# Attention and routing stage of a two-layer kernel: hand-written instruction orders with an earlier routing, one activation table, pads split over two queues, first expert weights scaled by ScalarE

## The reference, cut to what matters

```python
q, k = softplus(q), softplus(k)                          # 16 heads of 8
kv  = cumsum(k[:, :, :, None] * v[:, :, None, :], axis=1)
num = einsum('zsD,zsDe->zse', q, kv)
den = sum(q * cumsum(k, axis=1), axis=-1, keepdims=True)
x   = x + gate * ((num / den) @ Wo.T + bo)               # residual sum
t   = h * rsqrt(mean(h*h) + eps) * norm_scale            # h: layer norm of x, modulated
top_v, top_i = top_k(t @ gate_w + gate_b, 2)             # routing
probs = softmax(top_v)
y   = sum over the two experts of probs * (swiglu(t @ w1 + b1) @ w2 + b2)
out = x + gate * (h + y)
```

## Time and profile before

| | |
|---|---|
| device time, median of 3 runs | 1131.31 us (1131.22 to 1132.76) |
| the profiled execution, first to last instruction | 1130.5 us |
| PE, DVE, ACT, POOL busy | 904.8, 863.6, 682.1, 563.3 us |

### The profile page before, as it was taken

The page is one execution under the profiler, slowest core; times in us unless marked ns, Lnnn a source line. Parts: engine busy times, 40 slices in busy tenths (PEclk is TensorE's granted clock), DMA queues, the critical chain, the costliest instruction groups (busy, mean ns, idle before and its releaser), DMA issues.

```text
span 1130.5 us, 21078 instructions
## 1 busy us (share of the span) xinstructions
PE 904.8 (80%) x6543; PEld 700.5 (62%) x6543; DVE 863.6 (76%) x2224; ACT 682.1 (60%) x1756; POOL 563.3 (50%) x567
## 2 busy tenths in 40 slices
PE   4997799279999949999999999942088888888820
PEld 4994377134445438888888888831077777777710
DVE  2776788789998866788999999955467777676748
ACT  1357510689996376688988987755055555555510
POOL 1121000656885224433888888856635655555530
PEclk9999899579999969999999999975589999999975
DMA  7000233123333132000101111111242222222148
GB/s 191 14 1 5 75 112 112 52 85 132 123 118 113 75 102 51 2 8 9 42 32 39 38 37 40 35 37 45 82 131 72 82 71 77 79 68 77 45 165 307
DMA packets 72002, 84.37 MB, mean 75 GB/s; under 512 B 18182, under 2 KB 59841, under 8 KB 69716
## 3 DMA queue, kind: packets, MB, share of 16 engines
q1 hardware_dynamic: 52564, 60.60, 17.1%
q0 software_dynamic: 8704, 18.11, 4.8%
q10 hardware_dynamic: 10624, 4.33, 1.4%
HBM read 59.33 MB, written 23.67 MB: 73 GB/s over the span
## 4 chain that ended last, share of the span: by engine, by line
PE 39%; DVE 9%; issue 5%; ACT 4%; another core or an unknown queue 3%; DMA 1%; SPq 1%; POOL 0%; DVEq 0%; ACTq 0%; POOLq 0%
PE ps L2086 9%; PE ps L2304 9%; PE ps L2102 3%; PE ps L2323 3%; DVE qk L2003 2%; PE ps L2077 1%; PE ps L2064 1%; PE ps L2051 1%; PE ps L2097 1%; PE ps L2191 1%; PE ps L2156 1%; PE ps L2145 1%; PE ps L2209 1%; DVE qk L2008 1%
## 5 line engine op out<-in xcount | busy, mean ns | idle before, releaser
L1399 POOL DMA_INDIRECT rows_of<-payb,posu x128 | 143.2, 1119 | 53.3 <-issue 28.7
L1390 POOL TENSOR_TENSOR kvb<-qk,v 128x1024 f32<-128x1024 f32 x64 | 126.4, 1980 | 86.4 <-DVE qk L1756 53.0
L1032 PE MATMUL ps<-masked,ew 128*128 128x512 f32 x256 | 129.6, 621 | 4.2 <-DVE masked L960 3.5
L2086 PE MATMUL ps<-con,kvb 128*128 128x128 f32 x1024 | 126.9, 278 | 0.0
L2086 PEld LDWEIGHTS ps<-con,kvb 128*128 128x128 f32 x1024 | 120.4, 193 | 0.7 <-issue 0.7
L1424 POOL DMA_INDIRECT parts<-h,dest x72 | 74.0, 1028 | 72.3 <-ACT h L1658 47.2
L1649 ACT ACTIVATE nrm<-qk 128x512 f32<-128x512 f32 x72 | 45.4, 630 | 101.3 <-DVE qk L2003 87.8
L1424 POOL DMA_INDIRECT parts<-gx,dest x72 | 73.6, 1022 | 55.0 <-ACT gx L1658 33.9
L960 DVE TENSOR_TENSOR masked<-f_t,wide 128x512 f32<-128x512 f32 x128 | 88.9, 712 | 9.2 <-PE ps L1032 8.9
L1732 DVE TENSOR_TENSOR qc<-ps,qk 128x1024 f32<-128x1024 f32 x64 | 77.9, 1217 | 18.1 <-PE ps L2086 17.7
L2304 PE MATMUL ps<-qd,ex 128*128 128x256 f32 x288 | 74.4, 405 | 18.0 <-ACT ex L1634 15.8
(11 more groups left out here) (355 smaller groups left out, 2444.1 us busy)
## 6 DMA issues: line engine op xcount, KB each, us to landing
wide<-hot_dram SPq DMA_DIRECT2D x16, 1024.0 KB, 4.6
kvb<-rows_of SPq DMA_DIRECT2D x72, 132.0 KB
toep<-taps_dram SPq DMA_DIRECT2D x16, 512.0 KB, 3.8
out_dram<-x_tok ACTq DMA_DIRECT2D x16, 256.0 KB, 5.6
rows<-rows_dram SPq DMA_DIRECT2D x16, 192.0 KB, 3.1
kvb<-parts SPq DMA_DIRECT2D x6, 512.0 KB, 7.2
rows<-rows_dram SPq DMA_DIRECT2D x16, 128.0 KB, 4.4
xg<-in_w_dram SPq DMA_DIRECT2D x1, 2048.0 KB, 9.7
```

Source lines behind the costliest of these rows:

```text
L1032: nc.tensor.matmul(ps[:, w % 2, :], ew0[:, e, :], masked[e % 4][:, :], start=False, stop=(e == E - 1)).then_inc(s["product"], 1)
L1390: nc.gpsimd.tensor_tensor(kv[g % KB][:, :, :].rearrange("p e (h d) -> p e h d", h=H), k_in, v_in, ALU.mult).then_inc(s["kv"], 1)
L1399: nc.gpsimd.indirect_dma_start(rows_of, bass.IndirectOffsetOnAxis(ap=posu[w % 2][:, slot, t:t + 1], axis=0), pay[w % PB][:, t, :], None).t ...
L2086: last = nc.tensor.matmul(cum(g)[:, e, :], kv[g % KB][:, e, :], k("upto"), start=True, stop=True)
```

## The change

1. The round loops of POOL, ACT, DVE and PE are replaced by orders that are written out call by call. Routing runs closer behind the residual sum: in a steady round DVE calls `residual`, `moments`, `shifted`, `modulated` and `gated` of the same window, and `logits` to `placed` of the window two before. POOL makes the four products of window w in a row and then the eight sends of window w - 4 in a row; sends begin behind window 4 (before: behind window 6).
2. PE's waits for the shared banks are counted from what has been issued (`issued[...]`); waits for `abs_q` and `abs_k` are added. ACT's `relu_queries` waits for `den` too, its `relu_keys` for `kv`, `st_ps` and `k1` in place of `red`.
3. ACT loads one activation table that holds Exp and Ln, `natural_log_exp_and_others`, at the start of the phase.
4. SP writes the pads of experts 0 to 3, ACT those of 4 to 7.
5. The scaling of the first weights goes from DVE's plan to ACT, as four instructions of 1024 numbers each in rounds of the attention; the numbers `beside` are made by DVE in a round of the attention (`numbers()`), and two instructions of the plan on the counts become one ahead of it.

```diff
-                    for e in range(E):
+                    for e in range(E // 2):          # SP
                         row = sp.value_load(counts[0:1, e:e + 1], ...)
...
-                    for n in range(B + 7):           # POOL
-                        send(n - 7, 6)
-                        products(n, 0)
-                        send(n - 7, 7)
-                        send(n - 6, 0)
-                        products(n, 1)
...
+                    products(13, 3); send(9, 0); send(9, 1); ... send(9, 7)
+                    products(14, 0); products(14, 1); products(14, 2); products(14, 3); send(10, 0); ... send(10, 7)
+                    products(15, 0); products(15, 1); products(15, 2); products(15, 3)
+                    send(11, 0); ... send(11, 7); send(12, 0); ... send(15, 7)
...
+                    def scaled_weights(q):           # ACT
+                        need(act, "experts", (2 + NF) * 16)
+                        act.wait_ge(s["weights"], 3 * 16)
+                        by_e = w1b1.rearrange("p (e i) -> p e i", i=WB)[:, 2 * q:2 * q + 2, 0:I2]
+                        nc.scalar.activation(by_e, by_e, ACT.Copy, scale=ns[:, :]).then_inc(s["scaled"], 1)
...
+                    nc.scalar.preload_act_table_set("natural_log_exp_and_others")
+                    norm0(0); norm0(1); feat(0); norm0(2); relu_queries(0); abs_queries(0); relu_keys(0); abs_keys(0); feat(1); norm0(3)
+                    relu_queries(1); exponentials(0); relu_keys(1); ones_added(0); values(0); logarithm(0); values(1); abs_queries(1); abs_keys(1)
...
+                    act.wait_ge(s["place"], 1)
+                    act.wait_ge(s["padrow"], 2)
+                    for e in range(E // 2, E):
+                        row = act.value_load(counts[0:1, e:e + 1], min_val=e * CAP, max_val=(e + 1) * CAP - SP)
+                        act.dma_start(rows_of[bass.ds(row, SP), :]..., far[:, :, :]).then_inc(s["pads"], 16)
...
+                    weighted(11, 3); weighted(12, 0)  # DVE, one steady round
+                    correction(13); divided(11); added(10); corrected(13); weighted(12, 1); softplus(13); residual(11); moments(11); logits(9)
+                    denominators(12); weighted(12, 2); first_cum(13); largest(9); shifted(11); chosen(9); states(13); modulated(11); prefixes(13)
+                    ranked(9); gated(11); placed(9); weighted(12, 3); weighted(13, 0)
...
-                    first_weights = w1b1.rearrange("p (e i) -> p e i", i=WB)[:, :, 0:I2]
-                    nc.vector.tensor_scalar(first_weights, first_weights, ns[:, :], None, ALU.mult)
...
-                            need(pe, "relu_k", upto_b(w))
-                            need(pe, "wo_t", upto_b(w - 2))
+                            need(pe, "abs_k", issued["keys"])
+                            need(pe, "relu_k", issued["keys"])
+                            need(pe, "wo_t", issued["projected"])
...
+                    # PE, one steady round and the last of the attention
+                    queries(15); sums(13, 3); sums(14, 0); turn_pay(11); reduced(13, 3); sums(14, 1); logits(11); projected(13); denominators(14); sums(14, 2); back(13)
+                    reduced(14, 0); spread(14); states(15); logits_back(11); reduced(14, 1); reduced(14, 2); first_cum(15); turn_pay(12); sums(14, 3)
+                    ranks(11); sums(15, 0); reduced(14, 3); sums(15, 1); projected(14); logits(12); denominators(15); back(14); sums(15, 2)
+                    spread(15); logits_back(12); reduced(15, 0); reduced(15, 1); turn_pay(13); sums(15, 3); logits(13); reduced(15, 2); ranks(12)
+                    logits_back(13); reduced(15, 3); projected(15); back(15); ranks(13); turn_pay(14); logits(14); logits_back(14); turn_pay(15)
+                    ranks(14); logits(15); logits_back(15); ranks(15)
```

392 lines of the change are left out of this document (238 added, 154 removed).

## The result

The changed kernel took 1176.93 us (median of 4, 1173.64 to 1182.69) against 1132.03 (1131.22 to 1136.47) of the kernel before: ratio 1.0364 (95% interval 1.0325 to 1.0403). It is 3.6% slower, not 2% faster. The traced execution took 1175.91 us, span 1174.1.

A forecast was written before the change was run, and what follows sets the result against it. PE was taken to bound the steady rounds at 20.50 us and a queue of sends the tail. A tail gain of 27.6 less 3.6 for waits gave 24.0: 1131.3 - 24.0 = 1107 us, range 1097 to 1121.

The forecast's parts named there:

- Waits in the steady rounds: Steady rounds: PE instructions now wait for fresh DVE results; 0.3 us a round, +3.6 us over 12 rounds.
- Rival A: Steady rounds: three more POOL sends held by 1.2 us beside DVE, 1.0 us a round, 12 us; 1116 us; chance 0.18.
- Rival C: DVE's rounds: four places wait in turn for ACT or PE, 2.4 us a round, 29 us; 1132 us; chance 0.07.
- Fill at nothing: Start of the phase: table loads saved against a later `softplus(0)`; taken as 0, bounds -2.5 to +3 us.
- The tail: Sends behind POOL's last product: 40 instead of 52, at 1.342 us each, 53.7 us; 27.6 us gained.
- if all find their positions ready: Tail: no send waits for positions; window 15's come 38 us behind the last product, needed at 42.9.
- T: End of POOL's last product, start of the tail; forecast 733.4 us, the same as before.
- Pads and plan: Behind the tail: split pads end at T + 53, level with the last send; plan, 13.6 us, ends at T + 51.6, hidden.
- Weights: ACT's rounds: four scaling instructions add 4.2 us in four rounds, where table loads are gone; effect nothing.
- One table: ACT: 40 table loads, 51 us, go; hidden in steady rounds, counted within the tail's waits, only the fill left, taken as 0.
- D: ACT: the table stays two, keeping 51 us of loads and part of the tail's waits; 1114 us; chance 0.03.
- Rival B: Tail: the chain to window 15's positions, not the send queue, sets pads, plan and start; 1110 to 1127 us; chance 0.17.

The follow-up runs named there:

- a_late: Changed kernel with all 128 sends moved behind the last product, payload and position buffers 16 windows deep; 20.5 us a round, ratio 1.0758 to the kernel before.
- a_stand: Changed kernel with three POOL clearings in place of each send in the rounds, all sends behind the last product; 25.0 us a round, 1278.0 us in all.
- b_blocks: Kernel before with only POOL's order changed: four products, then eight sends of the window seven rounds back; 27.1 us a round, ratio 1.0657.
- a_mixed: Changed kernel with only POOL's order changed: two sends of the window five rounds back behind each product; 22.7 us a round, ratio 1.0042.
- b_parts: Kernel before with one table load, two-queue pads, weights on ACT, `beside` in a round, shorter plan, none of the orders; ratio 0.9934, again 0.9954.
- a_fit: Changed kernel, POOL's order fitted to idle gaps: five sends behind the second product, three behind the fourth; ratio 0.9958 (21.1 us a round), again 1.0205 (25.3).

## Why the prediction was wrong, step by step

*What bounds the kernel* was read rightly, PE at 20.5 us a round and the tail as a queue of sends. But "three engines stand within about 1.2 us of one another" was taken as slack of 1.2 us, when it meant that a few microseconds lost on DVE have nowhere to go.

*Failed step: the steady rounds.* "Waits in the steady rounds ... Above: 1.0 us a round ... I take 0.3" was +3.6 us on a last product at 733.4; measured is 805.2, +71.8. It failed in two ways.

First, the step priced only waits at semaphores. The change also moved the sends into one block, and with it the products into unbroken pairs that fell where DVE had no use for them. a_late (20.5) against a_stand (25.0) shows that POOL's occupation alone costs the tight orders 4.5 us a round, without late completions; b_blocks (27.1) shows that POOL's order costs the loose ones 6.5, without them too; and a_mixed (22.7) against the changed kernel (27.1) that another order of POOL takes most of it back, with late completions in both. Rival A had the mechanism and the wrong side: I priced holds that make *sends* longer, at most 1.2 us three times, on POOL, which had play. What counted was products that hold *DVE*: 2 to 6.4 us at a time, often on an instruction of 0.15 us, on an engine with 1.6 us to spare and with PE's next matrix products waiting behind it. And PE, idle 4.65 us of the round, had a granted clock of 0.88 in it, 1.00 before.

Second, the rows of before already had late completions: the first trace of before shows them on the `reduced` sums from its first sends on, 1.8 us in a round and none before its first send at 537.6. I never compared the end of a PE group with the start of its reader. With the loose order they cost nothing, with the fitted tight order the last products of a trace with them and of one without lie 40 us apart, and in the changed kernel some 26 of DVE's 37 us of longer waits bear their marks. Rival C, "the tight orders wait in turn", named this exposure and gave it 0.07; its 2.4 us a round was still a third of what came. Its sign came: PE's `values` wait 27.5 us in all (440 to 800 us) for DVE's `first_cum`. Which share each of the two has in the 71.8 us stays open.

*Fill at nothing*: no run isolates it; the first product started at 424.2 instead of 421.4, inside the bound of 3.

*The tail*: 27.6 us forecast, 16.4 measured. The count (40 sends) and the pace were right: without its waits the tail is 64.4 - 12.5 = 51.9, 1.30 a send (forecast 1.342). (Of window 9 four sends, not "two", stood in the old tail; 4 + 48 are the 52 that the sum rightly uses.) Mis-sized was "if all find their positions ready": window 12's came 9.1 us late and window 14's 3.2, while window 15's, which I had checked, were in time (851.98 for 859.86). That was luck: they came 46.9 us behind the last product, not 38, and would have been late for the send at T + 42.9 had the queue not waited before. In the four traces of this kind without late completions the tail takes 54.5 to 55.8, window 15's positions are made 35.5 to 36.9 us behind the last product, and only window 12's first send waits over 0.6 us (1.3 to 3.6). There the forecast of the tail holds but for that one wait; what it had not reckoned with were the late completions.

*Pads and plan* hidden: right. Base to `meta` took 7.0 us instead of 13.6 forecast and 17.7 before, the last pad was issued by 858.0; the last send is the end of the chain. *Weights* at nothing: right but for 1 us (b_parts' rounds 20.8 against 20.6, one of them 21.8). *One table*: right, one load, and D is out. *Rival B*: its sign came, POOL idle before window 14's sends and more before window 12's, and window 15's positions were 9 us behind the T + 38; but pads and `meta` stayed ahead of the last send, so the tail still ended as a queue, 10.7 us longer than the 53.7 forecast.

## What to carry to other kernels

On a busy DVE, ask of every long GpSimd instruction which DVE instruction it meets, and how long GpSimd's unbroken run is: with two sends behind each product the longest hold shown was 2.88 us, with three products in a row 6.39. Don't expect to win by rewriting the held instruction: here the hold passed on each time. A trace in which a hold went shows it only if the sum over DVE's instructions went too. Give GpSimd extra work where a trace without it shows it idle, rather than in a block. And before tightening an order, compare ends of producers with starts of idle readers in the old trace: lateness that is free there is paid for in the tight one.

## What was not expected of the hardware

- A hold can last until an unbroken run of GpSimd products ends: 2.63 us (two), 4.15 (two), 6.39 (three), on instructions of 0.15 to 1.2 us; also on a conversion with one input (3.95). It doesn't always: beside four products in a row (8.71 us, a_stand) DVE's instructions took turns with them, 2.12 and 2.34 us each. What decides is open.
- With indirect sends going on, PE results of some instructions reach their readers 1 to 4.7 us behind their recorded end in the rounds, 0.03 us otherwise. They come in batches: in a_fit_again results that ended at 522.75 and 523.74 were both signalled at 525.84. On one and the same chip two sets of runs had none in the rounds and one had them, so it isn't the chip alone; what sets it is open. In the sets without, the experts' stage took 269 to 270 us in six traces, with them 304 to 316, and the whole kernel before 1073 instead of 1128 to 1138. That the late completions cause this is likely but not shown. Slower transfers don't cause it: the packets of the largest queue took 18.3% of 1067.0 us in a_fit and 16.8% of 1162.9 in a_fit_again, 195 us both.
- A send takes 0.96 us and the next starts 0.30 later; the three sends beside DVE's `added`, `corrected` and `softplus`, all on two SBUF tensors, took 1.80 to 1.98 in the round shown.
